# Moving the attention output stage ahead of the expert routing in a fused attention and mixture-of-experts kernel

## What is computed

```python
xn = layernorm(x)
# attention branch, 16 heads of 64
q, k, v = split(xn @ w_qkv.T + b_qkv)
q = silu(q);  k = softmax(k, axis=tokens)
kv  = einsum('bhnd,bhne->bhde', k, v)          # over all 4096 tokens
out = layernorm(einsum('bhnd,bhde->bhne', q, kv), ln_g, ln_b)
gate = sigmoid((xn @ w_g1.T + b_g1) @ w_g2.T + b_g2)
attn = (out * gate) @ w_out.T + b_out
# mixture of experts, 1 shared expert and 8 routed ones, top 2
probs = softmax(xn @ Wr);  gates = top2(probs) normalised, else 0
ffn = gelu(xn @ Wfc_s) @ Wproj_s + sum_e gates[:, e] * (gelu(xn @ Wfc[e]) @ Wproj[e])
x = x + attn + ffn
```

## Time and profile before

| what | value |
|---|---|
| runs shown | 5427.72, 5693.78, 5370.45 us; median 5427.72 |
| the profiled execution | 5307.27 us |
| its span on the slowest core (7) | 5305.7 us |
| spans of the eight cores | 5300.6 to 5305.7 us |
| TensorE busy | 4761.4 us (90%) |
| VectorE, ScalarE, GpSimd busy | 822.7, 997.9, 160.8 us |
| chain that ended last: TensorE | 86% |
| mean granted TensorE clock | 0.938 to 0.939 of full speed |

### The profile page before, as it was taken

The page is one execution under the profiler, slowest core; times in us unless marked ns, Lnnn a source line. Parts: engine busy times, 40 slices in busy tenths (PEclk is TensorE's granted clock), DMA queues, the critical chain, the costliest instruction groups (busy, mean ns, idle before and its releaser), DMA issues.

```text
span 5305.7 us, 51642 instructions; the slowest of 8 cores (5300.6 to 5305.7 us)
## 1 busy us (share of the span) xinstructions
PE 4761.4 (90%) x20816; PEld 2056.9 (39%) x20816; DVE 822.7 (16%) x1358; ACT 997.9 (19%) x1472; POOL 160.8 (3%) x323
## 2 busy tenths in 40 slices
PE   3666665777999999999999999999999999999997
PEld 0212222223444444444444444444444444444443
DVE  1233333442000011010110101001010010101101
ACT  0111111222130211303112031120312203022130
POOL 0000000000000000000000000000000000000000
PEclk9777776778999999999999999999999999999999
DMA  5000002002444444444444444444444444444344
GB/s 119 0 1 8 8 0 40 1 0 48 72 79 74 78 79 77 80 80 75 81 75 80 74 82 79 77 80 76 79 81 76 80 77 79 80 75 81 74 79 112
DMA packets 53196, 344.24 MB, mean 65 GB/s; under 512 B 6690, under 2 KB 11298, under 8 KB 13538
## 3 DMA queue, kind: packets, MB, share of 16 engines
q0 software_dynamic: 46576, 314.87, 34.1%
q1 hardware_dynamic: 6386, 26.06, 1.5%
HBM read 647.31 MB, written 8.45 MB: 124 GB/s over the span
## 4 chain that ended last, share of the span: by engine, by line
PE 86%; DVE 7%; issue 2%; ACT 2%; SPq 1%; DMA 1%; DVEq 0%; ACTq 0%; POOL 0%; POOLq 0%
PE pb L749 19%; PE pb L754 19%; PE pb L709 19%; PE pb L715 19%; PE pb L225 2%; PE pb L220 1%; DVE xsq L270 1%; DVE s_sb L375 1%; PE pb L311 1%; PE pb L615 1%; PE pb L315 1%; PE pb L318 1%; PE pb L321 1%; PE pb L364 1%; SPq L189 1%
## 5 line engine op out<-in xcount | busy, mean ns | idle before, releaser
L749 PE MATMUL pb<-h_sb,ring 128*128 128x512 bf16 x4608 | 1746.4, 379 | 31.7 <-ACT h_sb L725 31.7
L709 PE MATMUL pb<-xn,ring 128*128 128x512 bf16 x4608 | 1747.4, 379 | 4.7 <-DMA ring<-wfc 4.0
L715 PE MATMUL pb<-xn,ring 128*128 128x512 bf16 x4608 | 1747.4, 379 | 0.0
L754 PE MATMUL pb<-h_sb,ring 128*128 128x512 bf16 x4608 | 1746.4, 379 | 0.0
L721 ACT ACTIVATE h_sb<-pb,bfc_sb 128x512 bf16<-128x512 f32 x576 | 395.7, 687 | 3055.7 <-PE pb L715 3055.6
L749 PEld LDWEIGHTS pb<-h_sb,ring 128*128 128x128 bf16 x4608 | 450.8, 98 | 581.6 <-issue 40.1
L709 PEld LDWEIGHTS pb<-xn,ring 128*128 128x128 bf16 x4608 | 451.1, 98 | 550.1 <-issue 7.2
L715 PEld LDWEIGHTS pb<-xn,ring 128*128 128x128 bf16 x4608 | 451.1, 98 | 543.9 <-issue 1.1
L754 PEld LDWEIGHTS pb<-h_sb,ring 128*128 128x128 bf16 x4608 | 450.8, 98 | 541.6
L774 DVE SCALAR_TENSOR_TENSOR gatec<-pb,bpj_sb,gbc 128x512 f32<-128x512 f32 x128 | 96.1, 751 | 3161.3 <-PE pb L754 3161.3
L725 ACT ACTIVATE h_sb<-pb,bfc_sb 128x512 bf16<-128x512 f32 x576 | 395.7, 687 | 54.3 <-ACT h_sb L721 1.5
(11 more groups left out here) (110 smaller groups left out, 1534.4 us busy)
## 6 DMA issues: line engine op xcount, KB each, us to landing
ring<-wfc POOLq DMA_DIRECT2D x144, 1024.0 KB, 9.9
ring<-wpj POOLq DMA_DIRECT2D x144, 1024.0 KB, 9.5
acc<-x_own SPq DMA_DIRECT2D x8, 1024.0 KB
gbc<-gate_dram SPq DMA_DIRECT2D x16, 512.0 KB, 8.4
out<-acc SPq DMA_DIRECT2D x8, 1024.0 KB
xo_bf<-x_oth POOLq DMA_DIRECT2D x4, 1024.0 KB, 35.8
wk_sb<-wk POOLq DMA_DIRECT2D x1, 2048.0 KB, 31.2
wv_sb<-wv POOLq DMA_DIRECT2D x1, 2048.0 KB, 46.2
```

Of the source, the lines that this page charges most:

```text
L709: op("tensor", lambda t, k=k, ml=ml, r=r, bka=bka, hf=hf: t.matmul(pb[bka][:], ring[r][:, k * 512 + ml * 128: k * 512 + ml * 128 + 128], x ...
L715: mm = op("tensor", lambda t, k=k, ml=ml, r=r, bkb=bkb, hf=hf: t.matmul(pb[bkb][:], ring[r][:, k * 512 + ml * 128: k * 512 + ml * 128 + 12 ...
L749: op("tensor", lambda t, m=m, r=r, bka=bka: t.matmul(pb[bka][:], ring[r][:, m * 128:(m + 1) * 128], h_sb[:, m * TH: m * TH + 512], start=( ...
L754: mm = op("tensor", lambda t, m=m, r=r, bkb=bkb: t.matmul(pb[bkb][:], ring[r][:, m * 128:(m + 1) * 128], h_sb[:, m * TH + 512: m * TH + 1024],
```

## The change

Stage 5, the whole output stage with `emit_q`, `qa = emit_q(0)`, the loop over four tiles and `p4_done = SV.n`, is cut out from between stage 4 and stage 6 and put between stage 3 and stage 4. Nothing inside it is altered, and nothing in the other stages. No instruction is added or taken away. The new order of every engine's queue is: keys/values, `kvbd`, loads of `wq_sb` and `wo_sb`, output stage, routing, gates to DRAM, experts.

```diff
     op("gpsimd", lambda g: g.dma_start(wo_sb, d_wo), inc=(SW2, 16))
     wo_tgt = SW2.n
 
+    def emit_q(tt):
+        t0 = tt * 512
+        qa = None
+        for qf in range(NCH):
...
+    qa = emit_q(0)
+    for tt in range(4):
+        t0 = tt * 512
+        aoe = None
...
+            ve = op("vector", lambda v, oc=oc, bk=bk, t0=t0: v.scalar_tensor_tensor(
+                acc[:, oc * T + t0: oc * T + t0 + 512], pb[bk][:],
+                bo_sb[:, oc:oc + 1], acc[:, oc * T + t0: oc * T + t0 + 512],
+                ALU.add, ALU.add), waits=[(SP, mm)], inc=(SV, 1))
+            bank_free[bk] = (SV, ve)
+
+    p4_done = SV.n
+
     lg_evac = None
     for tt in range(4):
         w0 = bw(0) + [xn_done]
@@ -532,99 +626,6 @@
             ALU.mult, ALU.mult),
             waits=[(SA, arc)] if tb == 0 else [], inc=(SV, 1))
 
-    def emit_q(tt):
...
-    qa = emit_q(0)
-    for tt in range(4):
...
-            bank_free[bk] = (SV, ve)
-
-    p4_done = SV.n
 
     for tb in range(16):
         bk = 1 + tb % 2
```

More of the change, by code:

```diff
@@ L461, in build_nc @@
     wo_tgt = SW2.n
-    lg_evac = None
-    for tt in range(4):
[L465 to L533, removed]
@@ L627, in build_nc @@
     p4_done = SV.n
+    lg_evac = None
+    for tt in range(4):
+        w0 = bw(0) + [xn_done]
+        mm = None
+        for hc in range(NCH):
+            mm = op("tensor", lambda t, hc=hc, tt=tt: t.matmul(
+                pb[0][0:8, :], wr_sb[:, hc * 8:(hc + 1) * 8],
+                xn[:, hc * T + tt * 512: hc * T + tt * 512 + 512],
+                start=(hc == 0), stop=(hc == NCH - 1)),
+                waits=w0 if hc == 0 else [],
+                inc=(SP, 1) if hc == NCH - 1 else None)
+        lg_evac = op("scalar", lambda s, tt=tt: s.copy(
+            lgt[:, tt * 512:(tt + 1) * 512], pb[0][0:8, :]),
+            waits=[(SP, mm)], inc=(SA, 1))
+        bank_free[0] = (SA, lg_evac)
@@ new lines, in build_nc @@
+    tr1 = None
+    for tb in range(16):
+        tr1 = op("tensor", lambda t, tb=tb: t.matmul(
+            pb[1][0:128, tb * 8:(tb + 1) * 8],
+            lgt[0:8, tb * 128:(tb + 1) * 128], ident[0:8, 0:8],
+            start=True, stop=True),
+            waits=(bw(1) + [(SA, lg_evac)]) if tb == 0 else [],
+            inc=(SP, 1) if tb == 15 else None)
+    ac_last = op("scalar", lambda s: s.copy(ltm5[:], pb[1][0:128, 0:128]),
+                 waits=[(SP, tr1)], inc=(SA, 1))
+    bank_free[1] = (SA, ac_last)
@@ new lines, in build_nc @@
+    vlast = None
+    for tb in range(16):
+        vlast = op("vector", lambda v, tb=tb: v.reduce_max(
+            nmx5[:, tb:tb + 1], ltm5[:, tb * 8:(tb + 1) * 8], axis=AX.X,
+            negate=True),
+            waits=[(SA, ac_last)] if tb == 0 else [], inc=(SV, 1))
+    alast = None
+    for tb in range(16):
+        alast = op("scalar", lambda s, tb=tb: s.activation(
+            e85[:, tb * 8:(tb + 1) * 8], ltm5[:, tb * 8:(tb + 1) * 8], AF.Exp,
+            bias=nmx5[:, tb:tb + 1]),
+            waits=[(SV, vlast)] if tb == 0 else [], inc=(SA, 1))
@@ new lines, in build_nc @@
+    for tb in range(16):
+        vlast = op("vector", lambda v, tb=tb: v.reduce_max(
+            m1c5[:, tb:tb + 1], e85[:, tb * 8:(tb + 1) * 8], axis=AX.X),
+            waits=[(SA, alast)] if tb == 0 else [], inc=(SV, 1))
+    for tb in range(16):
+        vlast = op("vector", lambda v, tb=tb: v.tensor_scalar(
+            nmk5[:, tb * 8:(tb + 1) * 8], e85[:, tb * 8:(tb + 1) * 8],
+            m1c5[:, tb:tb + 1], None, ALU.is_lt), inc=(SV, 1))
+    for tb in range(16):
+        vlast = op("vector", lambda v, tb=tb: v.tensor_tensor(
+            p2m5[:, tb * 8:(tb + 1) * 8], e85[:, tb * 8:(tb + 1) * 8],
+            nmk5[:, tb * 8:(tb + 1) * 8], ALU.mult), inc=(SV, 1))
@@ new lines, in build_nc @@
+    for tb in range(16):
+        vlast = op("vector", lambda v, tb=tb: v.reduce_max(
+            m2c5[:, tb:tb + 1], p2m5[:, tb * 8:(tb + 1) * 8], axis=AX.X),
+            inc=(SV, 1))
+    for tb in range(16):
+        vlast = op("vector", lambda v, tb=tb: v.tensor_scalar(
+            keep5[:, tb * 8:(tb + 1) * 8], e85[:, tb * 8:(tb + 1) * 8],
+            m2c5[:, tb:tb + 1], None, ALU.is_ge), inc=(SV, 1))
+    ad = op("gpsimd", lambda g: g.tensor_tensor(den5[:], m1c5[:], m2c5[:],
+                                                ALU.add),
+            waits=[(SV, vlast)], inc=(SGC, 1))
@@ new lines, in build_nc @@
+    vrd = op("vector", lambda v: v.reciprocal(rden5[:], den5[:]),
+             waits=[(SGC, ad)], inc=(SV, 1))
+    arc = op("scalar", lambda s: s.copy(nmx5[:], rden5[:]),
+             waits=[(SV, vrd)], inc=(SA, 1))
+    for tb in range(16):
+        vlast = op("vector", lambda v, tb=tb: v.scalar_tensor_tensor(
+            gtm5[:, tb * 8:(tb + 1) * 8], e85[:, tb * 8:(tb + 1) * 8],
+            nmx5[:, tb:tb + 1], keep5[:, tb * 8:(tb + 1) * 8],
+            ALU.mult, ALU.mult),
+            waits=[(SA, arc)] if tb == 0 else [], inc=(SV, 1))
```

## The result

Over 42 executions of each, the changed kernel takes 5340.2 us (median) and the kernel before 5307.1. The ratio is 1.0055, 95% interval 1.0042 to 1.0067: slower, by 29 us on the ratio and 33 us on the medians, and within 2%.

What follows compares the result with a forecast made beforehand. TensorE was taken to bound the experts, which the change leaves alone. Front -39.1 and back +58.1 gave +19 us, taken as +20 on the 5427.7 median: 5448 us, range 5333 to 5510.

Steps and rivals of the forecast that it cites:

- the base: Whole kernel: +20 us put on 5427.7, the median of the three runs shown, giving 5448 us.
- the gate transposes are unchanged: Between routing and experts: the gate transposes still take 13.2 us, on the path as before.
- no change: First expert matmuls: same low-clock start as before (0.51 for 3.6 us), despite about 40 us idle ahead; no cost.
- The front: From the last key/value product to the output stage's first product: 39.1 us earlier, with the `wq_sb` load the last wait.
- Rival 1: Front: the wait for `wq_sb` is 28.5 us, not 16.1; +32 in all, 5460 us; chance 0.05.
- The output stage: Output stage in its new place: same instructions and waits, still 332.5 us long.
- The routing at the back: Between output stage and experts: the whole routing chain is on the path, +58.1 us, or 63.8 with slow logits.
- The Exp table load: Routing at the back, ScalarE: one extra table load behind its instruction's wait, 1.28 us, without a drain.
- GpSimd's queue: Expert loads issued late in the routing: the first still has at least 6.5 us spare, so no cost.
- 2 (a late expert block): Start of the experts: first block lands after more than 19.2 us; +29, 5457 us; chance 0.03.
- 3 (something of the back hidden): Routing at the back: no more than 39.1 of 58.1 us shows, so not slower, about 5428 us; chance 0.08.
- 4 (the clock stays low): Experts: idle time leaves TensorE at its low clock for long; over 2% slower, 5530 us or more; chance 0.04.

Runs made afterwards that it cites:

- run 5: The changed kernel with `wo_sb` loaded first and `wq_sb` second; 5355.5 us (one run).
- run 9: The changed kernel with each routing batch of 16 tiny instructions fused into one; 5307.2 us, ratio to the kernel before 1.0009.
- run 1: The changed kernel with the first two expert loads issued right behind the output stage instead of in the routing; 5336.0 us.
- run 2: The changed kernel with only the first expert load issued right behind the output stage; four times at 5335 to 5338 us, the fifth 5380.
- run 3: The kernel before with its first two expert loads issued together about 7 us ahead of its first gate write; 5313.7 us, ratio 1.0013.
- run 6: The kernel before with one extra one-column ScalarE copy ahead of the experts; 5313.7 us, ratio 1.0007.
- run 7: The changed kernel with eight extra one-column ScalarE copies ahead of the experts; 5334.2 us (one run).

## Why the prediction was right or wrong

The direction and the mechanism were right, the size was short (+19 for +33 us), and the absolute time was wrong. Three steps failed: the base, "the gate transposes are unchanged", and "no change" in the experts.

- **The base.** The forecast of +20 us was put on 5427.7, the median of the runs shown, which gave 5448. That step failed and made the error: the base stands 121.6 us above the 5306.1 of the kernel before, the change was 13 us too small, and the two leave 5448 some 108 us too high. The prediction had noted that the runs differ by more than the change, and still chose their median. The better base was in its hands: the profiled execution with the change on it gave 5327, against 5339.5 of the one profiled after. That the measured 5340.2 lies inside the range of 5333 to 5510 is luck: the low end took the lowest of the three runs shown and went 57 us below it, by the distance between two of them. And 109 us was far too much for what a measurement can tell; with 42 executions of each the interval is 0.25% wide, or 13 us.
- **The front.** -39.1 forecast, -37.9 measured. `wq_sb` took 16.8 us instead of 16.1, and the 64 matmuls 16.58 instead of 16.1. That this load is what comes last is shown by run 5. Rival 1 (28.5 us) didn't happen by itself, and its price, 12.4 us, was near the 12.9 when run 5 forced it.
- **The output stage** kept its length (332.9 for 332.5), as forecast.
- **The routing at the back.** +58.1 forecast, 60.2 measured, all on the path (run 9). The logits went at full clock, 2.86 us from group to group for 2.7 forecast; the gap of 0.97 us counts from the end of the last matmul, so it comes on top of the group's 1.89 us and not of 8 x 0.216. The logit transposes took 5.23 instead of 4.33 us. The Exp table load was there, behind the wait of its instruction (ScalarE's timeline of the changed kernel):

```profile
1228.77 1.28 ACT L591 ACT_TABLE_LOAD   x1 [4.44 <-DVE nmx L585]
1230.07 5.80 ACT L591 ACTIVATE e<-ltm,nmx 128x8 f32<-128x8 f32 x15
```

  The exponentials begin 0.02 us behind it, without a drain, so the Trainium skill's further 1.38 us ("ScalarE: Activation LUTs", section "What ACT_TABLE_LOAD costs") does not show here either.
- **GpSimd's queue: the first term of the sum that failed.** The step asked whether the moved expert loads would be late for TensorE. They were not, as said. It did not ask whom they delay. SyncE's gate writes share the DMA engines with them, so the first of them landed in about 7 instead of 1.3 us, and the gate transposes, "13.2 us, are unchanged", took 20.1. Runs 1 to 3 show it from both sides, and the rows of the two DMA queues show the write standing still while the loads fill the engines. The rows for it were at hand: the issue 19 us ahead of the first expert matmul, the 13.2 us of writes inside those 19, and about 16 us for 2048 KB.
- **The experts: "No change" failed by 3.2 us.** The added table load, which was costed at its 1.28 us, also shifted all later ScalarE instructions by one place (runs 6 and 7). That alone costs 6.5 us on core 7, five waits and three stretches at 1.2 GHz; eight more instructions (run 7) took 5.9 us of the experts away again. The table shows 3.2 us because the experts also started slower (0.6 us) and TensorE waited 3.8 us less for weight blocks. No row of the kernel before could have given that size; the 1.76 us wait 18 times was there to be seen as the place where a small delay falls on TensorE. The clock falls behind some of the longer waits and not behind others, which makes part of the difference between cores; the waits for weight blocks (0.4 to 4.0 us per core in the kernel before) make another part.
- **Rivals.** 2 (a late expert block) did not happen, though its cause, two loads in a row beside other traffic, did harm elsewhere. 3 (something of the back hidden) is refuted by run 9. 4 (the clock stays low) is refuted: the experts' slow start lasted 4.6 us (1287.7 to 1292.3) against 3.6 before.

## What to carry to other kernels

Before moving a stage, ask what each idle stretch was covering: here one stretch of idle TensorE hid a weight load and most of a routing chain, and the move uncovered both and closed neither. Ask of every transfer that moves with it not only who waits for it, but whose small transfers it will stand in front of. And when a chain is made of many tiny instructions, fusing them beats rearranging them: it was worth 32 us in either order, while the rearrangement cost 33.

## What the runs showed of the hardware that was not expected

- A write of 4 KB from SyncE's queue took about 1.3 us alone, and about 7 us when 2 MB from GpSimd's queue had been issued 7 us before; in the changed kernel its first packet moved only 4.9 us after its issue. With 1 MB issued the same 7 us ahead (run 2) it was late by up to 1.1 us, and by nothing on cores 7 and 0.
- ScalarE has pauses of about 0.28 us at places fixed by the count of instructions ahead, recurring here every fourth expert half. One more instruction moved them onto TensorE's wait on all eight cores (run 6), eight more moved them off (run 7). What the engine does in them no run shows.
- A TensorE wait of 2.04 us in otherwise dense work was followed in 23 of the changed kernel's 40 cases and in 22 of the 40 of run 6 by some 3.4 us at 1.2 GHz, at 0.427 us from matmul to matmul instead of 0.216. Behind the waits of 1.76 to 1.98 us for Gelu it never was, in these two runs, the kernel before and run 7. Waits for a weight block went both ways: one of 2.24 us in the kernel before (core 7) was not followed by it, one of 2.26 us in run 6 (core 2) was.
